# Attention inside one fused transformer kernel: V's products in five groups a pair instead of seven, a packed buffer for the turned probabilities, and a new order of the pair

## The chip, the cores and the metric

One core of a Trainium2 chip runs the whole program. The metric is device time in microseconds (us); lower is better. Engines: PE (TensorE) multiplies and transposes, ACT (ScalarE) does exponentials and copies, DVE (VectorE) does row extremes, rotations and copies, POOL (GpSimd) does wide additions, SP (SyncE) only issues DMAs. Each engine runs its own list of instructions in order and waits for the others through semaphores.

## The reference, cut to what matters

Half a feed-forward block, attention, half a feed-forward block, each behind a layer norm, on 4 sequences of 1024 tokens of width 128. The change touches the attention alone (16 heads of 64, causal, rotary):

```python
q = apply_rotary_emb(q, cos, sin)
k = apply_rotary_emb(k, cos, sin)
scores = jnp.einsum('bhid,bhjd->bhij', q, k) * scale
scores = jnp.where(causal, scores, -jnp.inf)
probs = jax.nn.softmax(scores, axis=-1)
out = jnp.einsum('bhij,bhjd->bhid', probs, v)
out = jnp.einsum('btd,od->bto', out.reshape(...), wo)
```

## The kernel before, in words

**The pair.** Attention runs over 32 pairs: one pair is two heads of one sequence. A loop body holds two pairs, u = 0 and u = 1; the first carries in addition the projection of V for the next four heads (`ahead_v`, four steps of six matmuls). The queries of a pair are taken in two groups of row blocks: g = 0 with blocks 0, 1, 6, 7 and g = 1 with blocks 2, 3, 4, 5; each group has eight score units (4 blocks, 2 heads). In the text `score(p,1,k)` is a unit of the running pair's group 1, `next_score(k)` one of the next pair's group 0.

**From scores to V.** PE writes the scores of a unit into a wide PSUM tile (L725, L726), DVE masks them and takes the row extreme (`max_of`, L1008), ACT takes the exponential and the row sum (`exponential`, L904). The probabilities are then transposed on PE (`turn(p,g,t)`, ten turns a group, L742) into one of two PSUM banks, the ring; ACT copies each turn into the SBUF tile `turned`, which lies in `shared_a` (`keep_turned`, L915), and V is multiplied with it (`times_v(p,...,g,d)`, L759). A product for key block j takes two matmuls, one a head, each with its 64 columns of the array, with as many moving columns as there are row blocks that see key block j. In the trace each such matmul has two rows, so that a pair of key blocks shows as x8. A ring bank is written again only when its last reader has released it (`may_write`, semaphore `ring_free`).

**Groups of products.** `times_v` is called seven times a pair: (0,0) to (0,3) for g = 0 with two key blocks each, (1,0) to (1,2) for g = 1.

**The row sums.** DVE inverts the sums (`invert`), PE transposes them (`turn_sums`, L768), ACT copies them to `inv_rows` (`keep_sums`, L923), SP writes them to DRAM (`send_inv`, L1183), waits for that, and reads them back spread over 64 partitions a head (`spread_inv`, L1191). DVE multiplies the output with them (`normalise`).

**Queries and keys two pairs ahead.** `ahead(0)` to `ahead(5)` project q and k of the pair after the next one (L120 to L122). DVE rotates each (`rope`), POOL adds and splits the halves, and SP, in the following pair, carries them by DMA to the tiles the scores read: `may_fill`, sixteen DMAs for `q_hl` and `k_hh` (L179, L180), `send_inv(p,0)`, two DMAs for `k_low` (L185). `next_score(0)` waits for all of these.

**SP's list.** It is strictly in order. In a pair: the sixteen fills, `send_inv(p,0)`, two `k_low` fills, `spread_inv(p,0)`, V and output weights; then, behind the end of `ahead(5)`, the weights `w_qk`, in pairs with u = 1 also `w_v` and the 1024 KB of `xn_cur`; then `send_inv(p,1)`, `spread_inv(p,1)`; then the next pair's fills.

The order of all engines in a pair is written by hand, one `pair` function for each engine.

Of the kernel before, what the change touches and what calls it, by code (L numbers as in the profile page):

```python
# [15 lines left out]
TOKENS = BATCH * SEQ  # L16
# [4 lines left out]
P = 128  # L21
# [4 lines left out]
ALL_PAIRS = BATCH * PAIRS  # L26
# [17 lines left out]
def some(count):  # L44


    return not isinstance(count, int) or count > 0
# [558 lines left out]
def attention(nc, x, xn_dram, xn_stored, inv_dram, wo_pairs, ahead_of, o, constants,  # L606
# [5 lines left out]
    with ctx:  # L612
# [20 lines left out]
        NK = sum(KEYS)  # L633
        TURNS = [[(0, (0,)), (0, (1,)), (1, (0,)), (1, (1,))] + [(j, (0, 1)) for j in range(2, 8)],
                 [(j, (h,)) for j in range(4) for h in range(2)] + [(4, (0, 1)), (5, (0, 1))]]
        RING = [[0, 1, 2, 3, 4, 5, 7, 9, 10, 11], [12, 13, 14, 15, 16, 17, 18, 19, 21, 23]]
        RING_SUM, RING_OUT = [6, 20], [22, 8]
# [5 lines left out]
        turned = turned_mem[:].rearrange("p (s c) -> p s c", s=4)  # L643
# [26 lines left out]
        def rows_at(g, j):  # L670
            return [r for r, block in enumerate(TILES[g]) if block >= j]

# [21 lines left out]
        def _(pe):  # L694
# [51 lines left out]
            def times_v(p, i, u, g, d):  # L746
                if d == 0:
                    if g == 0:
                        pe.wait_ge(v_copied[u], 16 * (i + 1))
                    if some(2 * p + g):  # L750
                        pe.wait_ge(head_done, 2 * p + g)
                ats = [at for at, (j, heads) in zip(RING[g], TURNS[g]) if j // 2 == d]
                for b in sorted({at % 2 for at in ats}):
                    pe.wait_ge(ring_free[b], bank_count(p, max(at for at in ats if at % 2 == b)))
                for j in (2 * d, 2 * d + 1):
                    w = P * len(rows_at(g, j))
                    slot = (NK * u + KEYS[0] * g + j) % 4
                    for h in range(2):
                        last = nc.tensor.matmul(out_bank[HEAD_DIM * h:HEAD_DIM * (h + 1), CHUNK - w:],  # L759
                                                v_cur[:, u, j, HEAD_DIM * h:HEAD_DIM * (h + 1)],  # L760
                                                turned[:, slot, h * w:(h + 1) * w], start=(j == 0), stop=(j == KEYS[g] - 1))
                    last.then_inc(out_step, 1)
# [14 lines left out]
            def pair(i, u, first, last):  # L777
                p = 2 * i + u
                has_prev, has_next, has_next2 = not (first and u == 0), not (last and u == 1), not last

                def ahead(n):
                    if has_next2:
                        project(i + 1, u, n)

                def ahead_v(n):
                    if has_next2 and u == 0:
                        project_v(i + 1, n)

                def next_score(k):
                    if has_next:  # L790
                        score(p + 1, i + u, 1 - u, 0, k)
                    elif k < 2:
                        if k == 1:
                            pe.wait_ge(early.centred_done, 1)
                        early_mean(nc, early, k, x, proj_bank)
                    elif k in (2, 4):
                        if k == 2:
                            pe.wait_ge(early.centred_done, 2)
                        else:
                            pe.wait_ge(early.ln_done, 1)  # L800
                        early_variance(nc, pe, early, k // 2 - 1, proj_bank)

                score(p, i, u, 1, 0)
                turn(p, 0, 0)
                turn(p, 0, 1)
                score(p, i, u, 1, 1)
                turn(p, 0, 2)
                ahead(0)
                if has_prev:
                    times_v(p - 1, i - 1 + u, 1 - u, 1, 2)  # L810
# [4 lines left out]
                turn_sums(p, 0)  # L815
                score(p, i, u, 1, 3)
                ahead(1)
                score(p, i, u, 1, 4)
# [66 lines left out]
            times_v(ALL_PAIRS - 1, ALL_PAIRS // 2 - 1, 1, 1, 2)  # L885
# [3 lines left out]
        def _(act):  # L889
# [17 lines left out]
            def keep_turned(p, u, g, t, signals=1):  # L907
                j, heads = TURNS[g][t]
                at, w = RING[g][t], P * len(rows_at(g, j))
                act.wait_ge(ring_full, ring_count(p, at))  # L910
                if some(NK * p + KEYS[0] * g + j - 3):
                    act.wait_ge(out_step, NK * p + KEYS[0] * g + j - 3)
                slot = (NK * u + KEYS[0] * g + j) % 4
                to = slice(heads[0] * w, (heads[-1] + 1) * w)
                nc.scalar.activation(turned[:, slot, to], ring[at % 2][:, 0:w * len(heads)],  # L915
                                     ACT.Copy).then_inc(ring_free[at % 2], signals)
# [8 lines left out]
            def pair(i, u, first, last):  # L925
                p = 2 * i + u
# [16 lines left out]
                keep_turned(p, u, 0, 1)  # L943
                exponential(p, 1, 0)
                keep_turned(p, u, 0, 2)
                exponential(p, 1, 1)
                keep_turned(p, u, 0, 3)
                keep_turned(p, u, 0, 4)
                keep_sums(p, 0, 1 if has_prev else 2)
                exponential(p, 1, 2)  # L950
                exponential(p, 1, 3)
                keep_turned(p, u, 0, 5)
# [5 lines left out]
                keep_turned(p, u, 0, 8)  # L958
                keep_turned(p, u, 0, 9)
                exponential(p, 1, 7)  # L960
                keep_turned(p, u, 1, 0)
                keep_turned(p, u, 1, 1)
                next_exponential(0)
                keep_turned(p, u, 1, 2)
                keep_turned(p, u, 1, 3)
# [11 lines left out]
                ahead_v(1)  # L977
                ahead_v(2)
                keep_turned(p, u, 1, 9)
                next_exponential(5)  # L980
                next_exponential(6)
                ahead_v(3)
# [12 lines left out]
        def _(dve):  # L995
# [16 lines left out]
            def keep_turned(p, u, g, t, signals=1):  # L1012
# [3 lines left out]
                if some(NK * p + KEYS[0] * g + j - 3):  # L1016
                    dve.wait_ge(out_step, NK * p + KEYS[0] * g + j - 3)
                slot = (NK * u + KEYS[0] * g + j) % 4
                to = slice(heads[0] * w, (heads[-1] + 1) * w)
                nc.vector.tensor_copy(turned[:, slot, to], ring[at % 2][:, 0:w * len(heads)]).then_inc(ring_free[at % 2], signals)  # L1020
# [22 lines left out]
            def pair(i, u, first, last):  # L1043
# [16 lines left out]

                max_of(p, 1, 0)
                max_of(p, 1, 1)
                invert(p, 0)
                ahead(0)
                max_of(p, 1, 2)
                if has_prev:
                    normalise(p - 1, 1)
                max_of(p, 1, 3)
# [6 lines left out]
                max_of(p, 1, 6)  # L1075
                max_of(p, 1, 7)
                ahead(3)
                invert(p, 1)
                next_max(0)
                ahead(4)  # L1080
                next_max(1)
                next_max(2)
                ahead(5)
# [5 lines left out]
                next_max(6)  # L1089
                next_max(7)  # L1090
# [335 lines left out]
```

## Time and profile before

| | |
|---|---|
| median of 3 runs | 1266.02 us (1262.96 to 1270.62) |
| profiled execution | 1268.34 us, of which the span shown is 1266.6 us |
| PE busy | 1221.1 us, 96% of the span |
| ACT, DVE, POOL busy | 891.7, 747.8, 405.3 us |
| POOL's three steps for one half of q and k (L153, L1133, L164), mean | 2.39, 1.04, 2.38 us |
| granted TensorE clock, mean | 0.990 |

A row of the timeline gives the start of an instruction, its duration, engine, line, operation and tiles. Matmuls are pipelined: the next one starts before the last one's modelled end, so a matmul's price is the distance from its start to the next start, not its duration. What stands in brackets is idle time before the instruction and what ended it.

### The profile page before, as it was taken

How to read it: one execution, taken by the hardware profiler on the slowest of the kernel's cores; microseconds unless marked ns; L12 is line 12 of the kernel's file. 1: busy time of each engine (PE TensorE's matmuls, PEld its weight loads, DVE VectorE, ACT ScalarE, POOL GpSimd, SP SyncE). 2: the span in 40 equal slices, each digit the busy share in tenths (PEclk: the TensorE clock that was granted, in tenths of full speed). 3: DMA queues.
4: the chain of work that ended last, by engine and by line, in shares of the span. 5: the costliest groups of instructions: out<-in, count | busy, mean ns of one | idle time of the engine just before them, and what ended most of it. 6: DMA issues, size and time to landing. Idle time of an engine off the chain costs nothing. (4 is left out here: it accounts for less than half of the span.)

```text
span 1266.6 us, 26505 instructions
## 1 busy us (share of the span) xinstructions
PE 1221.1 (96%) x7264; PEld 843.2 (67%) x7264; DVE 747.8 (59%) x1789; ACT 891.7 (70%) x1945; POOL 405.3 (32%) x224
## 2 busy tenths in 40 slices
PE   6996899999999999999999999999999999999898
PEld 3554577767677767777777767676767676766465
DVE  5575656565656565666566565656565656564454
ACT  4665577777777777777777777777777777777564
POOL 4134423333333333333333233333232333330000
PEclk8998899999999999999999999999999999999999
DMA  7125555545555555555555564656555455543000
GB/s 277 58 99 141 159 130 138 140 140 136 141 143 140 141 138 142 137 140 147 127 150 144 128 166 119 168 127 168 127 144 142 134 137 141 142 101 78 11 34 34
DMA packets 118608, 164.86 MB, mean 130 GB/s; under 512 B 14385, under 2 KB 64433, under 8 KB 118449
## 3 DMA queue, kind: packets, MB, share of 16 engines
q1 hardware_dynamic: 118176, 163.70, 48.4%
q10 hardware_dynamic: 400, 0.79, 0.3%
q8 instruction: 14, 0.23, 0.1%
q14 instruction: 18, 0.14, 0.0%
HBM read 53.02 MB, written 10.75 MB: 50 GB/s over the span
## 5 line engine op out<-in xcount | busy, mean ns | idle before, releaser
L1008 DVE CUSTOM_DVE_ANT_0 probs<-wide,tri_mask 128x1024 f32<-128x1024 f32 (+7 forms) x512 | 382.5, 755 | 249.2 <-PE wide L726 245.7
L904 ACT ACTIVATE probs<-probs,neg_max 128x1024 f32<-128x1024 f32 (+7 forms) x512 | 394.6, 772 | 85.1 <-DVE neg_max L1008 83.1
L915 ACT ACTIVATE shared_a<-bank 128x512 f32<-128x512 f32 (+2 forms) x640 | 338.2, 549 | 164.3 <-PE bank L742 158.4
L742 PEld LDWEIGHTS bank<-ident,probs 128*128 128x128 f32 x2304 | 259.3, 140 | 132.2 <-issue 70.1
L742 PE MATMUL bank<-ident,probs 128*128 128x128 f32 x2304 | 343.5, 278 | 1.1 <-ACT shared_a L915 0.4
L153 POOL TENSOR_TENSOR rotated<-terms,cross 128x1024 f32<-128x1024 f32 x62 | 148.4, 2394 | 610.8 <-DVE cross L147 610.6
L759 PE MATMUL bank<-shared_a,v_cur 128*64 128x256 f32 (+3 forms) x1792 | 297.3, 453 | 0.0
L725 PE MATMUL wide<-k_hh,q_hl 128*128 128x512 f32 (+3 forms) x768 | 287.8, 377 | 6.2 <-DMA k_low<-parts 4.6
L726 PE MATMUL wide<-k_low,q_hl 128*128 128x512 f32 (+3 forms) x768 | 254.8, 344 | 0.0
L759 PEld LDWEIGHTS bank<-shared_a,v_cur 128*64 128x64 f32 x1792 | 108.8, 136 | 121.9 <-issue 85.2
L725 PEld LDWEIGHTS wide<-k_hh,q_hl 128*128 128x128 f32 x768 | 145.9, 190 | 34.2 <-issue 21.8
L164 POOL TENSOR_TENSOR parts<-rotated,parts 128x1024 fp32r<-128x1024 f32 x64 | 152.3, 2380 | 9.5 <-ACT parts L158 0.5
L726 PEld LDWEIGHTS wide<-k_low,q_hl 128*128 128x128 f32 x768 | 146.5, 191 | 10.1
L904 ACT ACTIVATION_READ_ACCUMULATOR probs<-probs,neg_max 128x1 f32 x512 | 97.7, 191 | 0.0
L120 PE MATMUL bank<-xn_cur,w_qk 128*128 128x256 f32 (+1 forms) x192 | 70.4, 367 | 12.2 <-PEq L246 8.7
L1133 POOL CAST parts<-rotated 128x1024 fp32r<-128x1024 f32 x62 | 64.4, 1038 | 23.5 <-DMA k_low<-parts 13.6
L1040 DVE TENSOR_TENSOR x<-bank,x 128x256 f32 (+1 forms) x32 | 13.6, 425 | 95.4 <-PE bank L775 71.4
L775 PE MATMUL bank<-head_out,wo_cur 128*128 128x512 f32 x128 | 65.5, 593 | 1.2 <-DVE head_out L1031 1.2
L1037 DVE TENSOR_TENSOR x<-bank,x 128x512 f32 (+1 forms) x32 | 22.1, 692 | 68.1 <-PE bank L775 68.1
L122 PE MATMUL bank<-xn_cur,w_qk 128*128 128x256 f32 (+1 forms) x192 | 61.9, 322 | 0.0
L121 PE MATMUL bank<-xn_cur,w_qk 128*128 128x256 f32 (+1 forms) x192 | 61.5, 320 | 0.0
L299 PE MATMUL bank<-shared_a,w_down 128*128 128x512 f32 x96 | 50.0, 615 | 10.0 <-DVE shared_a L480 10.0
(142 smaller groups left out, 1257.0 us busy)
## 6 DMA issues: line engine op xcount, KB each, us to landing
q_hl<-parts SPq DMA_DIRECT2D x254, 128.0 KB, 2.8
k_hh<-parts SPq DMA_DIRECT2D x254, 128.0 KB, 2.7
v_cur<-shared_b SPq DMA_DIRECT2D x32, 512.0 KB, 4.3
inv_sum<-inv_scratch SPq DMA_DIRECT2D x128, 128.0 KB, 3.3
k_low<-parts SPq DMA_DIRECT2D x63, 256.0 KB, 4.1
xn_cur<-xn_scratch SPq DMA_DIRECT2D x15, 1024.0 KB, 7.0
w_qk<-w_scratch SPq DMA_DIRECT2D x32, 256.0 KB, 3.1
w_scratch<-first_w_parts SPq DMA_DIRECT2D x8, 512.0 KB, 3.1
```

Of the source, the lines that this page charges most:

```text
L120: nc.tensor.matmul(out[:, 0:w], w_qk[:, 0, half], xn_cur[:, 0, xs], start=True, stop=False)
L153: unit.tensor_tensor(o.rotated[:], o.terms[:], o.cross[:], ALU.add).then_inc(o.sum_done, 1)
L164: nc.gpsimd.tensor_tensor(o.parts[:, 1, :, cols], o.rotated[:], o.parts[:, 0, :, cols].bitcast(F32), ALU.subtract).then_inc(o.low_done, 1)
L725: nc.tensor.matmul(out, q, k_hh[u][h][:, keys], start=True, stop=False)
L726: last = nc.tensor.matmul(out, q, k_low[u][h][:, keys], start=False, stop=True)
L742: last = nc.tensor.transpose(ring[at % 2][:, col:col + P], probs[g][:, h, OFFSET[g][r] + j * P:OFFSET[g][r] + (j + 1) * P], ident[:])
L759: last = nc.tensor.matmul(out_bank[HEAD_DIM * h:HEAD_DIM * (h + 1), CHUNK - w:], v_cur[:, u, j, HEAD_DIM * h:HEAD_DIM * (h + 1)], turned[: ...
L775: nc.tensor.matmul(ring[at % 2][:], wo_cur[:, u, :], head_out[:], start=True, stop=True).then_inc(ring_full, 1)
L904: nc.scalar.activation(own, own, ACT.Exp, bias=neg_max[g][:, col], scale=-1.0, accum_out=sums[g][:, col]).then_inc(probs_done, 1)
L915: nc.scalar.activation(turned[:, slot, to], ring[at % 2][:, 0:w * len(heads)], ACT.Copy).then_inc(ring_free[at % 2], signals)
L1008: nc.vector.tensor_tensor_reduce(out=part_of_probs(g, k), in0=wide_banks[k % 2][:, x0:x1], in1=tri_mask[:, SEQ - (x1 - x0):], scale=1.0, s ...
L1133: nc.gpsimd.tensor_copy(o.parts[:, 0, :, cols], o.rotated[:]).then_inc(high_done, 1)
```

## The change

V's products are issued in five groups a pair: `GROUPS` gives for g = 0 the key blocks (0, 1), (2 to 5), (6, 7), for g = 1 (0, 1, 2), (3, 4, 5). The four equal slots of `turned` become places of each block's own width (`PLACE`), which lie from the other end of the tile in every second pair; `TAKEN` says how many products must be done before a place is written again. Three of the twenty copies of turned probabilities go from ACT to DVE. The order on PE, ACT and DVE is new.

```diff
+        GROUPS = [[(0, 1), (2, 3, 4, 5), (6, 7)], [(0, 1, 2), (3, 4, 5)]]
+        TAKEN = [[-3, -3, -4, 0, -1, -2, 1, 1], [2, 4, 6, 8, 9, 9]]
...
-        RING_SUM, RING_OUT = [6, 20], [22, 8]
+        RING_SUM, RING_OUT = [6, 20], [21, 8]
...
+        def place(u, g, j):
+            width = 2 * P * len(rows_at(g, j))
+            return PLACE[g][j] if u == 0 else TOKENS - PLACE[g][j] - width
...
-                for j in (2 * d, 2 * d + 1):
+                for j in GROUPS[g][d]:
                     w = P * len(rows_at(g, j))
-                    slot = (NK * u + KEYS[0] * g + j) % 4
+                    at = place(u, g, j)
```

PE's pair, from the running pair's score unit 6 of group 1 to the end of the next pair's early units, and then around the turned sums:

```diff
                 score(p, i, u, 1, 6)
-                times_v(p, i, u, 0, 1)
                 turn(p, 0, 8)
                 turn(p, 0, 9)
                 ahead(3)
                 score(p, i, u, 1, 7)
-                times_v(p, i, u, 0, 2)
                 turn(p, 1, 0)
                 next_score(0)
                 turn(p, 1, 1)
                 next_score(1)
+                times_v(p, i, u, 0, 1)
                 ahead(4)
                 turn(p, 1, 2)
                 turn(p, 1, 3)
-                times_v(p, i, u, 0, 3)
                 next_score(2)
                 ahead(5)
                 next_score(3)
+                times_v(p, i, u, 0, 2)
...
                 turn(p, 1, 7)
+                times_v(p, i, u, 1, 0)
                 turn_sums(p, 1)
-                times_v(p, i, u, 1, 0)
-                turn(p, 1, 8)
                 ahead_v(1)
                 project_out(p, i, u, 0, RING_OUT[0], p)
-                turn(p, 1, 9)
+                turn(p, 1, 8)
                 ahead_v(2)
                 next_score(6)
+                turn(p, 1, 9)
                 next_score(7)
-                times_v(p, i, u, 1, 1)
                 ahead_v(3)
```

ACT's pair around the copy of the sums, and DVE's pair at two of its three new copies:

```diff
+                next_exponential(3)
+                ahead_v(0)
+                keep_turned(p, u, 1, 7)
                 keep_turned(p, u, 1, 6)
-                ahead_v(0)
-                next_exponential(3)
-                keep_turned(p, u, 1, 7)
+                ahead_v(1)
                 keep_sums(p, 1)
...
                 max_of(p, 1, 6)
+                keep_turned(p, u, 0, 8)
                 max_of(p, 1, 7)
...
+                keep_turned(p, u, 1, 3)
                 next_max(3)
                 normalise(p, 0)
+                ahead(5)
```

What stands in the rows below: L752 of the changed file is the transpose (L742 before), L735 and L736 the scores, L769 the products with V, L778 the turned sums; in the order a group's matmuls are counted once, not by their two rows in the trace.

On PE, just before the next pair's first score, the kernel before has this in the pair with u = 1 (the last score of the running pair, the group (0,2), `turn(p,1,0)`, `next_score(0)`):

```order
L725 MATMUL wide<-k_hh,q_hl 128x384
L726 MATMUL wide<-k_low,q_hl 128x384
L759 MATMUL bank<-shared_a,v_cur 64x256 x4
L731 REGISTER_ALU
L742 MATMUL bank<-ident,probs 128x128 x4
L716 REGISTER_ALU
L717 REGISTER_ALU
L718 ISA
L725 MATMUL wide<-k_hh,q_hl 128x512
L726 MATMUL wide<-k_low,q_hl 128x512
```

The changed kernel, from the wait of `turn(p,1,1)` on, has the products of four key blocks behind the next pair's second score:

```order
L747 REGISTER_ALU
L752 MATMUL bank<-ident,probs 128x128 x4
L735 MATMUL wide<-k_hh,q_hl 128x512
L736 MATMUL wide<-k_low,q_hl 128x512
L735 MATMUL wide<-k_hh,q_hl 128x384
L736 MATMUL wide<-k_low,q_hl 128x384
L769 MATMUL bank<-shared_a,v_cur 64x256 x8
L711 REGISTER_ALU
L120 MATMUL bank<-xn_cur,w_qk 128x256
```

Two groups of products, with 256 columns each, have moved from the stretch before `next_score(0)` to the stretch behind it.

On PE, late in the same pair, the kernel before transposes the sums ahead of the group (1,0):

```order
L742 MATMUL bank<-ident,probs 128x128 x3
L766 REGISTER_ALU
L731 REGISTER_ALU
L768 MATMUL bank<-ident,inv 128x128
L759 MATMUL bank<-shared_a,v_cur 64x512 x4
L742 MATMUL bank<-ident,probs 128x128 x4
```

and the changed kernel behind it:

```order
L752 MATMUL bank<-ident,probs 128x128 x3
L769 MATMUL bank<-shared_a,v_cur 64x512 x6
L776 REGISTER_ALU
L741 REGISTER_ALU
L778 MATMUL bank<-ident,inv 128x128
L785 MATMUL bank<-head_out,wo_cur 128x512
```

The group is longer by a key block, and the sums now come after it.

On DVE, between the extremes of the running pair's last two score units, a copy out of the ring has come in:

```order
L1012 ISA probs,neg_max<-wide,tri_mask 128x512
L1012 ISA neg_max 128x1
L1019 REGISTER_ALU
L1021 ISA
L1023 COPY shared_a<-bank 128x512
L1007 REGISTER_ALU
L1012 ISA probs,neg_max<-wide,tri_mask 128x384
```

This copy releases the ring bank that `turn(p,1,0)` writes next; before, it was ACT's.

## Rows read from the trace of the kernel before

**Rows 1.** PE's timeline, transposed sums (L768) of two pairs, 28 pairs apart.

```profile
181.79 0.30 PE L768 MATMUL bank<-ident,inv 128*128 128x128 f32 x1
1106.72 0.33 PE L768 MATMUL bank<-ident,inv 128*128 128x128 f32 x1
```

**Rows 2.** PE's timeline, groups of V's products and what stands beside them.

```profile
614.40 0.40 PE L725 MATMUL wide<-k_hh,q_hl 128*128 128x512 f32 x1
614.63 0.40 PE L726 MATMUL wide<-k_low,q_hl 128*128 128x512 f32 x1
614.96 1.08 PE L759 MATMUL bank<-shared_a,v_cur 128*64 128x256 f32 x8
615.98 0.88 PE L742 MATMUL bank<-ident,probs 128*128 128x128 f32 x6
...
621.33 0.60 PE L742 MATMUL bank<-ident,probs 128*128 128x128 f32 x4
621.68 0.48 PE L725 MATMUL wide<-k_hh,q_hl 128*128 128x512 f32 x1
...
629.77 1.94 PE L759 MATMUL bank<-shared_a,v_cur 128*64 128x512 f32 x8
631.64 0.66 PE L742 MATMUL bank<-ident,probs 128*128 128x128 f32 x4
632.05 0.36 PE L129 MATMUL bank<-w_v,xn_cur 128*128 128x256 f32 x1
...
632.85 1.02 PE L775 MATMUL bank<-head_out,wo_cur 128*128 128x512 f32 x2
```

**Rows 3.** PE's timeline over one loop body: end of ahead(5), sums, first scores.

```profile
592.86 0.28 PE L122 MATMUL bank<-xn_cur,w_qk 128*128 128x256 f32 x1
...
596.47 0.27 PE L768 MATMUL bank<-ident,inv 128*128 128x128 f32 x1
...
620.30 0.49 PE L725 MATMUL wide<-k_hh,q_hl 128*128 128x512 f32 x1 [0.79 <-DMA k_low<-parts]
...
625.28 0.28 PE L122 MATMUL bank<-xn_cur,w_qk 128*128 128x256 f32 x1
...
654.11 0.66 PE L742 MATMUL bank<-ident,probs 128*128 128x128 f32 x4
654.52 0.47 PE L725 MATMUL wide<-k_hh,q_hl 128*128 128x512 f32 x1
...
659.47 0.28 PE L122 MATMUL bank<-xn_cur,w_qk 128*128 128x256 f32 x1
...
685.86 0.47 PE L725 MATMUL wide<-k_hh,q_hl 128*128 128x512 f32 x1
```

**Rows 4.** SP's timeline in the same stretch: DMA issues.

```profile
597.33 0.27 SPq L1183 DMA_DIRECT2D inv_scratch<-inv_rows  x1
602.28 1.15 SPq L1191 DMA_DIRECT2D inv_sum<-inv_scratch  x2
604.12 0.59 SPq L179 DMA_DIRECT2D q_hl<-parts  x1
...
614.96 1.18 SPq L185 DMA_DIRECT2D k_low<-parts  x2
...
630.60 0.29 SPq L1183 DMA_DIRECT2D inv_scratch<-inv_rows  x1
631.87 1.14 SPq L1191 DMA_DIRECT2D inv_sum<-inv_scratch  x2
633.21 0.59 SPq L179 DMA_DIRECT2D q_hl<-parts  x1
```

**Rows 5.** DVE's timeline, extreme of the unit score(p,1,6).

```profile
651.27 0.68 DVE L1008 CUSTOM_DVE_ANT_0 probs<-wide,tri_mask 128x512 f32<-128x512 f32 x1
```

**Rows 6.** Busy time by stretch: us, then busy time by engine, granted clock, DMA share, GB/s.

```profile
136.00:140.00 4.00, 3.22 (x11) 2.50 (x9) 1.93 (x7) 0.99 (x4) 3.82 (x2) 0.57 0.59 172
949.00:955.00 6.00, 4.78 (x35) 3.93 (x35) 3.81 (x8) 3.14 (x7) 3.43 (x2) 1.00 0.62 163
```

More of the change, by code:

```diff
@@ L642, in attention @@
         probs = [sb(f"probs{g}", [P, 2, WIDTH]) for g in range(2)]
-        turned = turned_mem[:].rearrange("p (s c) -> p s c", s=4)
+        turned = turned_mem[:]
         neg_max, sums = ([sb(f"{n}{g}", [P, 8]) for g in range(2)] for n in ("neg_max", "sums"))
@@ L671, in rows_at, with steps_before @@
             return [r for r, block in enumerate(TILES[g]) if block >= j]
+        def place(u, g, j):
+            width = 2 * P * len(rows_at(g, j))
+            return PLACE[g][j] if u == 0 else TOKENS - PLACE[g][j] - width
+        def steps_before(p, g, j):
+            return NK * p + TAKEN[g][j]
         def unit(p, g, k):
@@ L751, in times_v @@
                         pe.wait_ge(head_done, 2 * p + g)
-                ats = [at for at, (j, heads) in zip(RING[g], TURNS[g]) if j // 2 == d]
+                ats = [at for at, (j, heads) in zip(RING[g], TURNS[g]) if j in GROUPS[g][d]]
                 for b in sorted({at % 2 for at in ats}):
                     pe.wait_ge(ring_free[b], bank_count(p, max(at for at in ats if at % 2 == b)))
-                for j in (2 * d, 2 * d + 1):
+                for j in GROUPS[g][d]:
                     w = P * len(rows_at(g, j))
-                    slot = (NK * u + KEYS[0] * g + j) % 4
+                    at = place(u, g, j)
                     for h in range(2):
@@ L760, in times_v @@
                                                 v_cur[:, u, j, HEAD_DIM * h:HEAD_DIM * (h + 1)],
-                                                turned[:, slot, h * w:(h + 1) * w], start=(j == 0), stop=(j == KEYS[g] - 1))
+                                                turned[:, at + h * w:at + (h + 1) * w], start=(j == 0), stop=(j == KEYS[g] - 1))
                     last.then_inc(out_step, 1)
@@ L804, in pair @@
                 turn(p, 0, 0)
+                score(p, i, u, 1, 1)
                 turn(p, 0, 1)
-                score(p, i, u, 1, 1)
                 turn(p, 0, 2)
@@ L809, in pair @@
                 if has_prev:
-                    times_v(p - 1, i - 1 + u, 1 - u, 1, 2)
+                    times_v(p - 1, i - 1 + u, 1 - u, 1, 1)
                 turn(p, 0, 3)
@@ L814, in pair @@
                 turn(p, 0, 5)
-                turn_sums(p, 0)
                 score(p, i, u, 1, 3)
                 ahead(1)
+                turn_sums(p, 0)
                 score(p, i, u, 1, 4)
@@ L910, in keep_turned @@
                 act.wait_ge(ring_full, ring_count(p, at))
[L911 to L915, printed above, removed]
+                if some(steps_before(p, g, j)):
+                    act.wait_ge(out_step, steps_before(p, g, j))
+                to = slice(place(u, g, j) + heads[0] * w, place(u, g, j) + (heads[-1] + 1) * w)
+                nc.scalar.activation(turned[:, to], ring[at % 2][:, 0:w * len(heads)],
                                      ACT.Copy).then_inc(ring_free[at % 2], signals)
@@ L948, in pair @@
                 keep_turned(p, u, 0, 4)
+                keep_turned(p, u, 0, 5)
                 keep_sums(p, 0, 1 if has_prev else 2)
@@ L951, in pair @@
                 exponential(p, 1, 3)
-                keep_turned(p, u, 0, 5)
                 exponential(p, 1, 4)
@@ L976, in pair @@
                 keep_turned(p, u, 1, 8)
-                ahead_v(1)
                 ahead_v(2)
-                keep_turned(p, u, 1, 9)
                 next_exponential(5)
+                ahead_v(3)
                 next_exponential(6)
-                ahead_v(3)
             for k in range(7):
@@ L1015, in keep_turned @@
                 dve.wait_ge(ring_full, ring_count(p, at))
[L1016 to L1020, printed above, removed]
+                if some(steps_before(p, g, j)):
+                    dve.wait_ge(out_step, steps_before(p, g, j))
+                to = slice(place(u, g, j) + heads[0] * w, place(u, g, j) + (heads[-1] + 1) * w)
+                nc.vector.tensor_copy(turned[:, to], ring[at % 2][:, 0:w * len(heads)]).then_inc(ring_free[at % 2], signals)
             def invert(p, g):
@@ L1075, in pair @@
                 max_of(p, 1, 6)
+                keep_turned(p, u, 0, 8)
                 max_of(p, 1, 7)
-                ahead(3)
                 invert(p, 1)
                 next_max(0)
+                ahead(3)
+                next_max(1)
                 ahead(4)
-                next_max(1)
                 next_max(2)
-                ahead(5)
+                keep_turned(p, u, 1, 3)
                 next_max(3)
                 normalise(p, 0)
+                ahead(5)
                 next_max(4)
@@ L1089, in pair @@
                 next_max(6)
+                keep_turned(p, u, 1, 9)
                 next_max(7)
```

15 lines of the change are left out of this document (7 added, 8 removed).

## The prediction, made before the changed kernel was run

> **What bounds the kernel now.** The mean period of a loop body (two pairs) comes first: 28 pairs, 14 bodies, take 1106.72 - 181.79 = 924.9 us, 66.07 us a body [rows 1]. Next I read PE's timeline through one body and marked two events: the last matmul of `ahead(5)`, call it X, and the first matmul of `next_score(0)`, call it N. In order they are X (u = 1) at 592.86, N (u = 0) at 620.30, X (u = 0) at 625.28, N (u = 1) at 654.52, X at 659.47, N at 685.86 [rows 3]. So a body has four stretches: A, from X of u = 1 to N of the next body; 4.98 us; B, 29.24 us; 4.95 us. The last three add up to 39.17, which leaves 66.07 - 39.17 = 26.90 for A on average.
>
> The N that closes A is the one that waits. In the first A it stood for `k_low`; that A took 27.44 us, the second, which waits for nothing, 26.39 [rows 3]. So PE alone would need 26.39 + 39.17 = 65.56 a body, the N that waits costs 0.5 more, and two paths of nearly equal length lead through A: PE's own work, and a chain of DMAs.
>
> That chain I read on SP's timeline [rows 4]. Behind X come the weights and `xn_cur`, then the sums go to DRAM at 597.33; their read-back is issued at 602.28 (4.95 us later, against 630.60 to 631.87, 1.27 us, in u = 0, where no `xn_cur` goes ahead of them); the first fill at 604.12; `k_low` at 614.96; N at 620.30. From the read-back to N is 18.02 us, of which 10.84 are the issuing of the sixteen fills. N - X on average less 18.02 puts the read-back 8.9 us behind X. The rest of the chain is SP's strict order, and nothing PE does makes it shorter.
>
> **The change part by part.** *Price of a group.* Two key blocks with 512 columns each take 631.64 - 629.77 = 1.87, two with 256 take 615.98 - 614.96 = 1.02 [rows 2]. The difference, 0.85, is two times 256 columns, so 0.85 is also what the columns of the shorter one cost, and 0.17 is the group's own. The matmul ahead of it takes 0.33 where its equal takes 0.23; four transposes behind it take 0.41 against 0.35 [rows 2]. That is 0.33; where a score follows, its second matmul is late as well, so I take 0.36. Two groups fewer: 0.72 a pair, 23 us over 32 pairs, if PE sets the pace.
>
> *Where the work goes.* Group (0,1) of the new division (four key blocks with 256 columns, 4 x 0.425 = 1.70) moves from before N to between N and X. Its last group, key blocks 6 and 7 (384 columns, 0.64), moves from there to behind X. So the two short stretches each grow by 1.06, to 6.04 and 6.01, while their number of groups stays one. A and B lose 1.06 of columns and two groups of six: 1.78 each. PE would reach N 24.6 us behind X in A, and take 27.5 in B.
>
> *The sums.* This is the step that I think decides. `turn_sums(p,1)` went behind the group (1,0), which has grown by a key block, and behind the group (0,2), which now lies after X. In A it stands 596.47 - 592.86 = 3.61 behind X now [rows 3]. Added: 384 columns and a group, 0.64 + 0.33; 3 x 512 columns and a group, 2.55 + 0.33. That makes 7.5. From the transpose to the DMA's issue took 0.86 (597.33 less 596.47), so the issue comes at 8.3, and with 1.27 for the way to DRAM the read-back at 9.6. In this body it was at 9.4, on average at 8.9: `xn_cur` covers most of the delay, not all. I take 9.5, so A = 9.5 + 18.0 = 27.5, where PE is ready at 24.6. PE then waits 2.9 us, less what other waits inside A take of it.
>
> In B nothing large goes ahead of the sums. There the transposed sums wait for `ahead_v(0)` too (six projections, 632.85 - 632.05 = 0.80 [rows 2]): 8.3 behind X. ACT now copies `ahead_v(1)` before the sums: another 0.80 and part of a copy, then 0.86. Issue at 9.9 to 10.4, I take 9.9; read-back 11.2; first fill 1.34 later (631.87 to 633.21); `k_low` 10.84 after that; N another 5.34 (614.96 to 620.30) [rows 3, 4]. That is 28.7, where PE would be ready at 27.5. A chain with slack now binds.
>
> *The copies that go to DVE.* ACT loses three, which is worth nothing, since no term above is ACT's work. The copy behind `score(p,1,6)` is new in front of `turn(p,1,0)`. DVE ends that unit's extreme at 651.95 [rows 5]; the copy itself has no row in this trace: the same engine's pass over 512 columns, 0.68, is the nearest, zero the other end. It would end by 652.6, while `turn(p,1,0)`, which starts at 654.11 behind two groups (2 x 1.18) that are gone, could start at 651.8 [rows 3]. So up to 0.8 of waiting, ahead of N in both halves. In A the DMA chain covers it; in B it lifts PE's 27.5 to 28.3, still under 28.7. If the chain in B were shorter, it would be the next in line. The copy in front of `next_max(3)`, with `normalise` ahead of the last `rope`, brings POOL's halves 1 to 2 us later; they must be there by the first fill, 11 us behind X, and an end of `rope` 3 us behind X leaves 8 for POOL, whose three steps take 5.8 (the table of the profile): no cost.
>
> *The places of `turned`.* Same columns, other addresses: nothing on PE, ACT or DVE. Its new waits name products that stand earlier in PE's order than the turns which they hold back: nothing.
>
> *Sum.* 27.5 + 6.04 + 28.7 + 6.01 = 68.25 us a body against 66.07: 2.2 more. Fourteen bodies make 30.5; the first and the last pair, without such a chain, give back 0.72 each. So +29 on the profiled 1268.34 (span 1266.6), and, since that stands 2.3 above the median of 1266.02, 1295 on the scale of the median.
>
> [...]
>
> **The rivals.** *PE sets the pace after all:* the groups' 0.72 a pair come out in full, 1266 - 23 = 1243. For it: PE is busy 96% of the span and N waits for only 0.5 a body. Against: A's chain, 26.9, is longer than PE's 26.4 today, and PE's road through A shrinks while work moves to the stretch behind N. It needs a chain that gets 2 us shorter.
>
> *The change doesn't do what it says, because A's chain keeps its length and B stays PE's:* 26.9 + 6.04 + 27.5 + 6.01 = 66.45, 0.4 a body, +4 with the ends: 1270. The saving in A is lost to the wait, and the one in B goes into the two stretches. For it: `xn_cur` may hide the late sums altogether.
>
> *Only one chain is late:* A at 27.5 and B at 27.5 make 67.05, +13 with the ends: 1279. It needs ACT to reach the sums in B 1.2 us sooner than I have it.
>
> *The waits cost clock:* worst of all, on the slower side beyond mine. At 131 to 140 us, where PE stands for stretches of up to 3 us, the granted clock of 136 to 140 is 0.57, near the lower of its levels (1.2 of 2.4 GHz); in 949 to 955, with the longest wait at N, it is 1.00 [rows 6]. Fourteen waits of up to 2.9 us lie between. If each brought 4 us at 0.57, 1.7 of work would be lost each time, 24 in all: 1319. The Trainium skill (TensorE: Matmul & The Clock Gate, HAM oscillation) says that waits for DMA between bursts of matmuls can do this; here only the start of the program shows it.
>
> **How the numbers follow.** Both chains late 0.64, at 1295, its own range 1284 to 1308. One chain late 0.13. Chain unchanged 0.08. PE's pace 0.08. Clock lost 0.07. The range 1267 to 1308 leaves out the fast case, the clock case and little else. A measurement of this kernel can tell a change of about 0.5%, 6.3 us, from none: faster 0.08, same 0.08 (1270 lies in it), slower 0.84.
>
> **What would show it.** In the trace of the changed kernel N should carry a wait for `k_low` in every body, of 2 us or more at u = 0 and of up to 1 at u = 1; the sums should be sent 8 us behind X instead of 4.5; the read-back should follow 1.3 us later; X to N should be 27 to 28 and 28 to 29 us, and a body 68. There should be five groups a pair, each with the same 0.17 of its own. `turn(p,1,0)` should wait for DVE. I am wrong if N starts without waiting, if the read-back follows X in less than 9 us, or if the body's period falls below 66.

## The result and the profile after

The changed kernel takes 1313.28 us (median; 1305.93 to 1319.97) against 1265.53 for the kernel before: ratio 1.037, 95% interval 1.034 to 1.041. The direction was right; the time is 18.3 us above the forecast and 5 above its range. The profiled execution took 1305.93 us (span 1304.2).

PE's timeline in the profiled execution: sums of two pairs, 28 pairs apart, then X and N over one body, as in [rows 1, 3].

```profile
178.61 0.27 PE L778 MATMUL bank<-ident,inv 128*128 128x128 f32 x1
...
606.29 0.28 PE L122 MATMUL bank<-xn_cur,w_qk 128*128 128x256 f32 x1
...
613.63 0.33 PE L778 MATMUL bank<-ident,inv 128*128 128x128 f32 x1
...
633.55 0.49 PE L735 MATMUL wide<-k_hh,q_hl 128*128 128x512 f32 x1 [1.13 <-DMA k_low<-parts]
...
639.60 0.28 PE L122 MATMUL bank<-xn_cur,w_qk 128*128 128x256 f32 x1
...
668.34 0.49 PE L735 MATMUL wide<-k_hh,q_hl 128*128 128x512 f32 x1
...
674.69 0.28 PE L122 MATMUL bank<-xn_cur,w_qk 128*128 128x256 f32 x1
...
702.09 0.49 PE L735 MATMUL wide<-k_hh,q_hl 128*128 128x512 f32 x1 [1.28 <-DMA k_low<-parts]
...
1138.55 0.27 PE L778 MATMUL bank<-ident,inv 128*128 128x128 f32 x1
```

| us | before | forecast | after |
|---|---|---|---|
| A, X (u = 1) to N | 26.9 mean | 27.5 | 27.3, N waits |
| N to X (u = 0) | 4.98 | 6.04 | 6.05 |
| B, X (u = 0) to N | 29.24 | 28.7 | 28.74, N does not wait |
| N to X (u = 1) | 4.95 | 6.01 | 6.35 |
| body | 66.07 | 68.25 | 68.4 in most; mean of 14, (1138.55 - 178.61)/14 = 68.57 |

The row to look at is N at 668.34: it has no bracket. A is closed by the DMA, as forecast; B is closed by PE.

SP's timeline of the same body, as in [rows 4].

```profile
614.29 0.27 SPq L1189 DMA_DIRECT2D inv_scratch<-inv_rows  x1
615.54 1.15 SPq L1197 DMA_DIRECT2D inv_sum<-inv_scratch  x2
617.38 0.59 SPq L179 DMA_DIRECT2D q_hl<-parts  x1
...
628.22 1.18 SPq L185 DMA_DIRECT2D k_low<-parts  x2
...
649.49 0.29 SPq L1189 DMA_DIRECT2D inv_scratch<-inv_rows  x1
650.77 1.13 SPq L1197 DMA_DIRECT2D inv_sum<-inv_scratch  x2
652.10 0.59 SPq L179 DMA_DIRECT2D q_hl<-parts  x1
...
662.95 1.18 SPq L185 DMA_DIRECT2D k_low<-parts  x2
```

In A the sums go 614.29 - 606.29 = 8.0 behind X and the read-back 9.25 (forecast 8.3 and 9.5), in B 9.9 and 11.2 (forecast 9.9 and 11.2). From `k_low` to N are 633.55 - 628.22 = 5.33 in A; in B the same 5.34 would give 668.29, and PE is there at 668.34. So B's chain is as long as forecast, but PE arrives with it and not 0.4 to 1.2 earlier.

What delays PE stands in the groups of the profile's page (columns: busy time and mean ns; idle time before them, and what ended most of it):

```profile
L735 PE MATMUL wide<-k_hh,q_hl 128*128 128x512 f32 (+3 forms) x768 | 293.9, 383 | 22.5 <-DMA k_low<-parts 20.6
...
L120 PE MATMUL bank<-xn_cur,w_qk 128*128 128x256 f32 (+1 forms) x192 | 74.3, 387 | 25.5 <-DVE cross L147 13.4
```

The first line is the forecast wait at N (6.2 before). The second wasn't forecast: `ahead(3)` stands for DVE, some 30 times. DVE's timeline there:

```profile
664.56 0.69 DVE L1040 TENSOR_TENSOR x<-bank,x 128x512 f32 x1 [2.13 <-PE bank L785]
665.17 0.81 DVE L1012 CUSTOM_DVE_ANT_0 probs<-wide,tri_mask 128x640 f32<-128x640 f32 x1
...
665.91 0.42 DVE L146 TENSOR_TENSOR cross<-bank,cos 128x256 f32<-128x256 f32 x1
666.25 0.41 DVE L147 SCALAR_TENSOR_TENSOR cross<-bank,sin 128x256 f32<-128x256 f32 x1
666.58 0.68 DVE L1012 CUSTOM_DVE_ANT_0 probs<-wide,tri_mask 128x512 f32<-128x512 f32 x1
...
667.18 0.69 DVE L1023 COPY shared_a<-bank 128x512 f32<-128x512 f32 x1
```

Behind `project_out` DVE has 3.3 us of work without a gap: the addition to x, a maximum, `ahead(2)`'s rope, a maximum, the new copy. All projections share one bank, so `ahead(3)` can't start before the rope of `ahead(2)` has read it (666.6). In the kernel before, the group (0,1) [rows 2, 614.96 to 615.98] stood between the two, and needs nothing of DVE. That group is what the change carries behind N.

*Where the 48 us are.* The first X and the last, in the profile before, in the one after, and in that of a second series of the changed kernel:

```profile
163.44 0.28 PE L122 MATMUL bank<-xn_cur,w_qk 128*128 128x256 f32 x1
...
1122.63 0.28 PE L122 MATMUL bank<-xn_cur,w_qk 128*128 128x256 f32 x1
```

```profile
158.52 0.28 PE L122 MATMUL bank<-xn_cur,w_qk 128*128 128x256 f32 x1
...
1153.55 0.28 PE L122 MATMUL bank<-xn_cur,w_qk 128*128 128x256 f32 x1
```

```profile
164.49 0.28 PE L122 MATMUL bank<-xn_cur,w_qk 128*128 128x256 f32 x1
...
1160.52 0.28 PE L122 MATMUL bank<-xn_cur,w_qk 128*128 128x256 f32 x1
```

The third execution (1313.23 us, span 1311.5) stands for the median. Against the one before: 1.0 us up to the first X, 996.0 - 959.2 = 36.8 between the marks (14.5 bodies), and 151.0 - 144.0 = 7.0 behind the last X; together the 44.9 by which it is longer than 1268.34. The profiled execution is shorter chiefly by its start, 6.0 us: there the granted clock is 0.91 in its first 40 us and from 130 to 150, where the third has 0.87 and 0.74.

### The profile page after: what moved, and what is told of

Same layout as the page of the kernel before. It is cut to its first block and busy times, and to the rows that moved or that the text cites. A ratio compares the mean times of both kernels' runs of the same rounds, so it can differ in the third digit from the quotient of the medians.

```text
span 1304.2 us, 26489 instructions
## 1 busy us (share of the span) xinstructions
PE 1223.6 (94%) x7264; PEld 851.3 (65%) x7264; DVE 801.8 (61%) x1885; ACT 847.1 (65%) x1849; POOL 405.5 (31%) x224
## 5 line engine op out<-in xcount | busy, mean ns | idle before, releaser
L922 ACT ACTIVATE shared_a<-bank 128x512 f32<-128x512 f32 (+2 forms) x544 | 291.3, 555 | 154.6 <-PE bank L752 150.3
L752 PE MATMUL bank<-ident,probs 128*128 128x128 f32 x2304 | 342.0, 278 | 6.7 <-DVE x L1044 3.2
L752 PEld LDWEIGHTS bank<-ident,probs 128*128 128x128 f32 x2304 | 261.1, 141 | 111.1 <-issue 43.8
L735 PE MATMUL wide<-k_hh,q_hl 128*128 128x512 f32 (+3 forms) x768 | 293.9, 383 | 22.5 <-DMA k_low<-parts 20.6
L769 PE MATMUL bank<-shared_a,v_cur 128*64 128x256 f32 (+3 forms) x1792 | 283.3, 449 | 1.8 <-DVE shared_a L1023 1.8
L736 PE MATMUL wide<-k_low,q_hl 128*128 128x512 f32 (+3 forms) x768 | 258.0, 344 | 0.0
L769 PEld LDWEIGHTS bank<-shared_a,v_cur 128*64 128x64 f32 x1792 | 114.5, 136 | 123.4 <-issue 92.3
L735 PEld LDWEIGHTS wide<-k_hh,q_hl 128*128 128x128 f32 x768 | 146.4, 191 | 39.1 <-issue 16.3
L736 PEld LDWEIGHTS wide<-k_low,q_hl 128*128 128x128 f32 x768 | 147.2, 192 | 10.0
L120 PE MATMUL bank<-xn_cur,w_qk 128*128 128x256 f32 (+1 forms) x192 | 74.3, 387 | 25.5 <-DVE cross L147 13.4
L903 ACT ACTIVATE shared_b<-bank 128x512 f32<-128x512 f32 x60 | 35.5, 592 | 50.0 <-PE bank L131 49.4
L120 PEld LDWEIGHTS bank<-xn_cur,w_qk 128*128 128x128 f32 x192 | 36.3, 189 | 47.1 <-DVE cross L147 20.7
L122 PE MATMUL bank<-xn_cur,w_qk 128*128 128x256 f32 (+1 forms) x192 | 62.0, 323 | 0.0
```

Source lines behind the costliest of these rows:

```text
L120: nc.tensor.matmul(out[:, 0:w], w_qk[:, 0, half], xn_cur[:, 0, xs], start=True, stop=False)
L735: nc.tensor.matmul(out, q, k_hh[u][h][:, keys], start=True, stop=False)
L736: last = nc.tensor.matmul(out, q, k_low[u][h][:, keys], start=False, stop=True)
L752: last = nc.tensor.transpose(ring[at % 2][:, col:col + P], probs[g][:, h, OFFSET[g][r] + j * P:OFFSET[g][r] + (j + 1) * P], ident[:])
L922: nc.scalar.activation(turned[:, to], ring[at % 2][:, 0:w * len(heads)], ACT.Copy).then_inc(ring_free[at % 2], signals)
```

## The experiments

All ratios are to the kernel before, run beside them. Medians of the kernel before were 1264.99, 1264.53 and 1264.61 in the three series.

**The changed kernel again**, unedited, for a second trace.

> The changed kernel once more, unchanged, to see how far its own executions lie apart. Its profiled execution had a body of 68.4 us, a granted clock of 1.00 inside the loop and 0.990 on average, and 1305.9 us; its other executions had mean clocks of 0.981 to 0.987 and 1311.9 to 1320.0 us. Theory (chains and waits, with some clock lost on top): times between 1305 and 1320, and the slower ones have the lower mean clock, about 1.3 us for each 0.001 of it. Rival (the spread is DMA latency alone): the mean clock does not go with the time. If a profiled execution here has less than 1.00 inside the loop, the stretch where it falls should lie behind N at u = 0, the longest wait of PE.

1313.81 us, 1.038 (1.035 to 1.041). As expected; its trace is used above.

**Sums back ahead of the group.**

```
  turn(p, 1, 7)
+ turn_sums(p, 1)
  times_v(p, i, u, 1, 0)
- turn_sums(p, 1)
```

> The changed kernel with one step undone: the sums of group 1 are transposed ahead of the group (1,0) again, and ACT copies them before the copy of ahead_v(1). Theory (the late sums make the chains late and hold up ACT at the end of the pair): the sums are sent about 5.5 us behind X instead of 8, A falls from 27.3 to about 26.8 (xn_cur then bounds the read-back), and the waits at the end of the u = 0 pair (0.14 and 0.40 us) go; 0.5 to 1.0 us a body, 7 to 14 us in all, 1299 to 1306. Rival (the late sums are covered and the cost sits in the groups and copies themselves): no change within 0.5%, 1307 to 1320.

1296.89 us, 1.026 (1.023 to 1.028); 17 less than the changed kernel, a little more than expected. ACT's copies were put in the matching order. A falls to between 25.9, without a wait at N, and 27.4; B from 28.74 to 28.56. So the late sums make about a third of the 48 us, and PE's own road through A is 25.9, not the 24.6 of the prediction. B's chain is early here. SP's timeline, and PE's at N:

```profile
656.64 1.18 SPq L185 DMA_DIRECT2D k_low<-parts  x2
```

```profile
664.29 0.48 PE L735 MATMUL wide<-k_hh,q_hl 128*128 128x512 f32 x1
```

With X at 635.74, `k_low` goes 20.9 behind X instead of 23.35, so with the 5.34 from there to N the chain would let N start at 26.2; it starts at 28.55. In this run PE, with its waits for DVE and ACT, closes B, and no DMA does.

**Late sums alone**, in the kernel before.

```
- turn_sums(p, 1)
  times_v(p, i, u, 1, 0)
+ turn_sums(p, 1)
```

> The kernel before with the turned sums behind the group (1,0) and nothing else. Theory, that xn_cur's transfer covers the delay until about 8 us behind X: the sums are sent 6.7 behind X instead of 4.5, the read-back stays at 9 to 9.5, A 26.5 to 27.4 and B 29.25 as before, time 1264 to 1270. Rival, that the chain grows by all of the delay: read-back at 11.1, A 29.1, time 1265 + 2.2 x 14.5 = 1297.

1281.60 us, 1.013 (1.010 to 1.016): between the two, and by neither mechanism. In A the read-back stays 7.7 to 9.5 behind X, as the first theory said, but A is 27.15 with N *not* waiting, and B grew from 29.25 to 29.74. PE's timeline behind the sums:

```profile
606.34 0.33 PE L768 MATMUL bank<-ident,inv 128*128 128x128 f32 x1
...
607.02 1.13 PE L775 MATMUL bank<-head_out,wo_cur 128*128 128x512 f32 x2
608.63 0.44 PE L742 MATMUL bank<-ident,probs 128*128 128x128 f32 x2 [0.48 <-ACT shared_a L915]
```

The transposed sums now meet the transposes behind them in the two turning banks, and PE waits for ACT's copies. A step in the strict order has two costs, the chain it starts and the bank it holds; I had priced the first.

**The sums on another queue**, in the kernel before: sent from ACT's queue, not behind `xn_cur`'s transfer on SP's.

```
  nc.scalar.activation(inv_rows[g][:], ...)
+ if g == 1:
+     act.wait_ge(ring_free[at % 2], bank_count(p, at))
+     act.dma_start(inv_dram[g], inv_rows[g][:]).then_inc(inv_sent[g], 16)
...
- send_inv(p, 1)
```

> The kernel before with one edit: the sums of group 1 go to DRAM from ACT's own DMA queue, right behind their copy, instead of from SP's, where they stand behind xn_cur. Theory (A is a chain of DMAs whose first link is the wait of the sums behind xn_cur): the read-back is issued about 6 us behind X instead of 8.9, or at the latest when the queue is free; fills start when POOL's halves are there, 7.5 to 8 us behind X; N no longer waits, the body is 65.6 instead of 66.1: 5 to 8 us less, 1258 to 1261. Rival (the queue does not matter, the DMA engines are shared): A stays at 26.9, 1266.

1262.45 us, 0.998 (0.996 to 1.000): not clear of the noise, where 5 to 8 us were expected. The trace shows what the time can't. ACT's and SP's timelines:

```profile
597.09 0.27 ACTq L926 DMA_DIRECT2D inv_scratch<-inv_rows  x1
```

```profile
600.50 1.15 SPq L1194 DMA_DIRECT2D inv_sum<-inv_scratch  x2
```

With X at 592.63 the read-back is 7.9 behind X (9.4 in [rows 4]); even on a queue of its own a 4 KB write takes 3.4 us to its read-back beside `xn_cur`'s transfer (3.2 to 4.5 over the bodies), against 1.27 in B. From the third body on A is 26.4 with no wait at N, the body 65.57. That is PE's own time of [rows 3], now in nearly every body.

**The changed kernel without its chain in A**: sums early and on ACT's queue.

> The changed kernel with the turned sums back ahead of the group (1,0) and the sums of group 1 sent from ACT's queue. Theory, that A is set by the DMA chain and that what is left of the loss is PE's waits for DVE and ACT: A 25.9 with 0 to 0.4 of waiting, B 28.56 as before, short stretches 6.05 to 6.37, body 66.9, time 1285 (1281 to 1289) against 1296.9 with the sums turned early alone; and if it is the waits at N that cost clock, the mean granted clock is 0.988 or more in each execution. Rival, that PE's other waits take what the wait at N gives back: 1294 to 1298.

1293.07 us, 1.022 (1.019 to 1.025); only 4 less than with early sums alone, not clear of the noise, and nearer the rival. But for the first body A is 26.0 to 26.5, yet the stretch behind N of u = 0, 6.05 before, is now up to 6.37: where N doesn't stand, `turn(p,1,1)` stands for the exponential instead. The expectation about the clock missed too: two executions of four are at 0.985 and 0.986. So with the chain gone the five groups are still 28 us slower than before, and what is left is PE waiting for DVE and ACT.

**Five groups in the old order**: (0,1) where (0,2) stood, ahead of N; (0,2) where (0,3) stood; the old (1,1) gone; the copies on ACT as before.

```
  score(p, i, u, 1, 6)
- times_v(p, i, u, 0, 1)
...
  score(p, i, u, 1, 7)
- times_v(p, i, u, 0, 2)
+ times_v(p, i, u, 0, 1)
...
- times_v(p, i, u, 0, 3)
+ times_v(p, i, u, 0, 2)
...
- times_v(p, i, u, 1, 1)
  ahead_v(3)
```

> The kernel before with the five groups and the packed, mirrored places alone; the order of everything else stays, (0,1) stands where (0,2) stood, ahead of N, (0,2) where (0,3) stood, the old (1,1) is gone. No copy goes to DVE. Theory: each group saves 0.36 us, so B shrinks from 29.25 to 28.5, the two short stretches stay at 4.97, and A stays with its DMA chain at about 26.9 while PE would be ready at 25.7; body 65.3, 0.75 less than before, 10 to 13 us: 1253 to 1256. Rival 1 (fewer groups are worth nothing, or packing costs): 1266 or more. Rival 2 (no chain, PE sets the pace): 23 us less, 1243.

1294.10 us, 1.024 (1.022 to 1.026) where 1253 to 1256 was expected: the clearest miss. PE's timeline at the place where the group is gone:

```profile
662.15 0.82 PE L752 MATMUL bank<-ident,probs 128*128 128x128 f32 x6
663.42 0.50 PE L120 MATMUL bank<-xn_cur,w_qk 128*128 128x512 f32 x1 [0.46 <-DVE cross L147]
```

The same `ahead(3)` in the kernel before, behind the six transposes at 615.98 in [rows 2]:

```profile
616.61 0.47 PE L120 MATMUL bank<-xn_cur,w_qk 128*128 128x512 f32 x1
```

663.42 - 662.15 = 1.27 for six transposes that take 616.61 - 615.98 = 0.63 there: 0.64 lost where the group saved 0.36. Similar waits, for DVE's maximum and ACT's exponentials, came where (1,1) stood. N does not wait in most bodies and the body is 67.9. Against PE's 65.56 that is 1.2 more a pair: two groups fewer took 0.72 off PE's work and brought some 1.9 of waits that they had hidden. The other half of rival 1, that packing costs, has no sign in the trace: between 300 and 1090 us neither ACT nor DVE waits for a product before it writes a place.

**The columns moved back ahead of N**, in the changed kernel: (0,1) behind `score(p,1,6)`, (0,2) between N and X.

```
  score(p, i, u, 1, 6)
+ times_v(p, i, u, 0, 1)
...
  next_score(1)
- times_v(p, i, u, 0, 1)
  ahead(4)
  turn(p, 1, 2)
  turn(p, 1, 3)
+ times_v(p, i, u, 0, 2)
...
  next_score(3)
- times_v(p, i, u, 0, 2)
```

> The changed kernel with the four-key group (0,1) back ahead of N (behind score(p,1,6)) and the last group (0,2) back between N and X. Theory, that N in A stands for the DMA chain and columns put behind N are paid in full, and that ahead(3) waits 0.65 us for DVE only because no products stand ahead of it: short stretches 4.97 and about 5.3 (from 6.06 and 6.35), A 26.6 to 27.0, B 28.74 + 2.06 - 0.97 - 0.65 = 29.2, body 66.2, time 1313.8 - 2.2 x 14.5 = about 1282 (1278 to 1286). Rival, that DMA chains decide A and B alike: A 26.9, B 28.6, body 65.5, time 1271. Rival, that the place of the columns is all one and the waits lie elsewhere: body 68.4, time 1311 to 1315.

1342.36 us, 1.062 (1.060 to 1.065): 29 worse than the changed kernel, where 32 better was expected, and outside both rivals. The short stretches are 6.7 to 7.1 although they lost columns. PE's timeline:

```profile
652.83 0.34 PE L736 MATMUL wide<-k_low,q_hl 128*128 128x384 f32 x1
654.63 0.39 PE L120 MATMUL bank<-xn_cur,w_qk 128*128 128x256 f32 x1 [1.47 <-DVE terms L143]
```

The change has also moved the rope of `ahead(3)` behind `next_max(0)`, and the group (0,1) in its new place is the cover of that rope; taken out, `ahead(4)` waits about 1.7 us in every pair. The columns behind N are not simply paid in full, as the prediction had it: they hide DVE there, as they did ahead of N.

**The rope ahead of the maximum**, on DVE in the changed kernel.

```
+ ahead(2)
  max_of(p, 1, 5)
- ahead(2)
```

> The changed kernel with one swap on DVE: the rope of ahead(2) goes ahead of max_of(p,1,5). Theory, that PE's own waits (ahead(3) for that rope, 0.65 us a pair) set B, and the DMA chain sets A: B 28.74 becomes 28.1, in A the wait at N grows from 1.4 to 2.0 and A stays 27.3, body 67.8, time 1313.8 - 0.65 x 14.5 = about 1304 (1302 to 1307). Rival, that a DMA chain sets B too, as forecast: nothing changes, 1311 to 1316.

1309.12 us, 1.036 (1.033 to 1.039), between theory and rival and hardly clear of the changed kernel. The wait of `ahead(3)` is gone, B is still 28.76 and the 4 us come from elsewhere (`turn(p,1,1)`; the last stretch is 6.07, not 6.35). PE's timeline in A; in B the same wait is 0.60:

```profile
632.06 0.48 PE L120 MATMUL bank<-xn_cur,w_qk 128*128 128x512 f32 x1
...
633.99 0.66 PE L752 MATMUL bank<-ident,probs 128*128 128x128 f32 x4 [0.59 <-DVE shared_a L1023]
```

This is `turn(p,1,0)` waiting for the copy on DVE, the step that the prediction named with "up to 0.8". In the changed kernel the wait of `ahead(3)` hides it: PE is held once, by DVE's 3.3 us, wherever it first asks. N does not wait in B, so what kept B is this wait. The rival, a chain in B, isn't ruled out by this run: the chain ends within 0.1 us of PE, and would have held N in its place.

**The copy behind `score(p,1,6)` back on ACT.**

> The changed kernel with the copy behind score(p,1,6) back on ACT. Theory: DVE has 0.3 us of idle time behind that copy and no instruction of PE waits for it there, so nothing changes: 1309 to 1317. Rival, the step of the prediction that this copy delays turn(p,1,0) by up to 0.8 us ahead of N: B 28.0 and 1302.

1318.88 us, 1.043 (1.040 to 1.047), 5 worse, where no change was expected. PE's timeline, u = 0:

```profile
640.15 0.66 PE L752 MATMUL bank<-ident,probs 128*128 128x128 f32 x4 [0.69 <-ACT shared_a L922]
...
641.19 0.49 PE L735 MATMUL wide<-k_hh,q_hl 128*128 128x512 f32 x1 [0.38 <-DMA k_low<-parts]
```

ACT is later with that copy than DVE, and `turn(p,1,0)` stands 0.8 us longer in both halves. This tells the two stretches apart: B went from 28.74 to 29.54, all of it (the stretch behind it gave 0.3 back), while A stayed at 27.27 and the wait at N shrank from 1.4 to 0.6. A is closed by the DMA chain. In B the chain is no later than PE; that PE closes B even without the chain is shown by the run with the sums back ahead, where `k_low` came 2.45 us earlier and B lost only 0.18.

**Four places put back together**: columns, sums, rope and queue.

> The changed kernel with four places put back: the four-key group ahead of N and the last group between N and X, the turned sums ahead of the group (1,0), the rope of ahead(2) ahead of max_of(p,1,5), and the sums of group 1 sent from ACT's queue. Theory (chain in A, PE's waits in B, ends some 7 us longer): A 26.3 without a wait at N, short stretches 5.0 and 5.3, B 29.0, body 65.6, time about 1266 (1262 to 1271). Rival, that fewer groups bring new waits of PE for ACT's copies at the seam of the pairs, as with the five groups in the old order: body 66.8 or more, 1283 or more.

1343.17 us, 1.064 (1.060 to 1.067), where about 1266 was expected. It has the fault of the columns run: `ahead(4)` waits for the rope of `ahead(3)`, and the short stretches are mostly 6.7 to 7.1. The time lies where the rival had it, but the wait is for DVE and not for ACT.

**Six groups**, in the kernel before with the sums on ACT's queue: blocks 2 to 5 as one group at the old place of blocks 2 and 3, so that `ahead(3)` keeps its cover.

```
+ GROUPS = [[(0, 1), (2, 3, 4, 5), (6, 7)], [(0, 1), (2, 3), (4, 5)]]
...
  score(p, i, u, 1, 7)
- times_v(p, i, u, 0, 2)
  turn(p, 1, 0)
...
- times_v(p, i, u, 0, 3)
+ times_v(p, i, u, 0, 2)
```

> The kernel before with one group fewer (key blocks 2 to 5 as one group, at the place of the old group of blocks 2 and 3, so that ahead(3) keeps its cover; group 1 keeps its three groups) and with the sums of group 1 sent from ACT's queue. Theory, that a group is worth 0.36 us where it covered no wait: body 65.57 - 0.72 = 64.85, N without a wait, time 1262.5 - 0.72 x 14.5 = about 1252 (1249 to 1256). Rival, that a group taken away brings a wait in its place wherever it stood, as in the five groups in the old order: 1260 to 1275.

1268.09 us, 1.003 (1.002 to 1.004). Where N doesn't wait, A and B lose 0.3 each, about as expected, and the short stretches gain 0.4; in other bodies A is up to 28.4 and N waits for `k_low` again. PE's timeline:

```profile
652.91 0.40 PE L727 MATMUL wide<-k_low,q_hl 128*128 128x512 f32 x1
653.52 0.55 PE L743 MATMUL bank<-ident,probs 128*128 128x128 f32 x3 [0.21 <-ACT probs L904]
```

The group that stood behind `score(p,1,7)` had covered the road from that score over its maximum and its exponential to `turn(p,1,1)`.

**Six groups, with a score put into the gap.**

```
  next_score(0)
- turn(p, 1, 1)
  next_score(1)
+ turn(p, 1, 1)
```

> The kernel before with six groups and with the sums of group 1 sent from ACT's queue, as in the run of that name, and turn(p,1,1) moved behind next_score(1). Theory, that the 0.4 us which the six groups lost behind N was turn(p,1,1) standing for score(p,1,7), its maximum and its exponential, which the group taken away had covered, and that a score now covers it: short stretches 4.97, A 26.1 plus up to 0.5 of waiting for the chain, B 28.95, body 64.9 to 65.3, time 1252 to 1258. Rival, that DVE sets the pace behind N and the wait moves on to ahead(4) or next_score(2): 1265 to 1269 as without the swap.

1260.44 us, 0.997 (0.996 to 0.999), over 12 runs; the body is 65.44. This is 0.3% faster than the kernel before, by 4 us where 7 to 13 were expected: 8 us of the wait came back, but A is 26.34, not 26.1, with 0.1 to 0.2 each of new waits for a maximum and a turning bank. It doesn't separate from the kernel with the other queue alone (1262.45, in another series), so that fewer groups gain anything in the time isn't shown.

## Why the prediction was wrong

*Price of a group: right, and no use alone.* The six groups took 0.3 out of A and of B, near the 0.36. The step that failed is the next one, "A and B lose 1.06 of columns and two groups of six: 1.78 each. PE would reach N 24.6 us behind X in A, and take 27.5 in B." It treats the products as work and not as cover. PE's road is 25.9 in A and 28.74 in B. For B the difference of 1.24 is three waits in the trace after: `ahead(3)` 0.70, `ahead_v(3)` for ACT's copy 0.40, `turn(1,8)` for the sums' copy 0.14. They don't simply add: with the last two all but gone (sums back ahead) B lost 0.18. Over a body in which nothing waits for a DMA, that run has PE at 25.91 + 6.35 + 28.56 + 6.35 = 67.2, where the prediction's figures for PE add up to 64.15 and the kernel before took 65.56: even with the sums back ahead the change makes PE's own road longer, not shorter. The profile before could have shown the first wait. DVE's timeline there, the last step of that rope:

```profile
615.68 0.42 DVE L147 SCALAR_TENSOR_TENSOR cross<-bank,sin 128x256 f32<-128x256 f32 x1
```

It ends at 616.1 and PE asks for it at 616.61, so 1.02 of products stand over 0.5 of slack.

*The sums in A: right*, to 0.3 us in each of their times, and A came out at 27.3 for 27.5. N waits 1.4 and not 2.9 (the prediction asked for 2 or more), because other waits inside A have taken the rest; the prediction allowed for that and the copy run shows it.

*B: right number, by luck.* The chain of 28.7 is there, but PE's 28.74 closes B, and N starts without waiting, which the prediction named as a sign of being wrong. With the chain 2.45 us earlier B is still 28.56. That the two meet within 0.1 us hid the failed step: the body came out at 68.4 for 68.25.

*N to X: right for u = 0* (6.05 for 6.04); for u = 1 0.34 short, `turn(p,1,1)` waiting for the exponential.

*The copy on DVE: right in kind.* Its wait of up to 0.8 exists, but is hidden behind that of `ahead(3)`, as the rope run shows.

*The ends: mis-sized.* "The first and the last pair, without such a chain, give back 0.72 each" was -1.4; behind the last X it is +7.0. The last loads have a chain too, and without projections PE has less to put beside it. PE's timeline there, in the profile after; the kernel before has neither wait:

```profile
1180.70 0.77 PE L735 MATMUL wide<-k_hh,q_hl 128*128 128x512 f32 x1 [2.66 <-DMA k_low<-parts]
...
1228.88 1.52 PE L769 MATMUL bank<-shared_a,v_cur 128*64 128x384 f32 x12 [1.77 <-DVE shared_a L1023]
```

The first is the last N. Behind it the granted clock is 0.57 from 1180 to 1182 and 0.58 from 1182 to 1184 us, some 1.7 of work lost; with the 2.66 and the 1.77 that is most of the 7.0. The longer end comes with the new order, the copies on DVE among it, and neither with five groups alone nor with the late sums: behind the last X there are 144.2 us with five groups in the old order, as before (144.0), and 151.7 with the sums back ahead.

*The sum.* Of the 18.3 us by which the time missed, 8.4 are the ends, 6.3 the stretch between the marks (36.8 for 30.5: bodies of 68.4, half a body more than counted, and first bodies of 69 to 71), 1.0 the start and 2.3 that I moved the sum down to the median's scale, which the changed kernel's traces don't follow.

*The clock rival (0.07) holds in single bodies.* Busy time by stretch in the rope run (us, busy by engine, granted clock, DMA share, GB/s):

```profile
428.00:430.00 2.00, 0.41 (x2) 0.38 (x3) 0.20 (x1) 0.89 (x3) 0.43 (x1) 1.00 0.84 247
430.00:432.00 2.00, 2.00 (x10) 1.72 (x9) 0.99 (x1) 0.00 (x0) 1.85 (x2) 0.67 0.97 228
432.00:434.00 2.00, 2.00 (x10) 1.09 (x10) 2.00 (x5) 1.66 (x3) 1.13 (x1) 0.50 0.00 0
434.00:436.00 2.00, 2.00 (x19) 1.32 (x16) 0.45 (x2) 0.06 (x1) 0.00 (x0) 0.98 0.00 0
```

PE stood 0.6 us ahead of `turn(p,1,0)` and 1.8 at N (429.58); then the clock is granted at 0.50, its lower level, and the stretch to X takes 7.65 instead of 6.07. The Trainium skill (TensorE: Matmul & The Clock Gate, HAM oscillation) has such a loss behind waits between bursts; this trace agrees, while the profile after holds 1.00 in the whole loop, through thirteen gaps ahead of N of 1.4 to 2.4 us. The second trace of the changed kernel, the run without the chain and the copy run have one such body each, the run of four places three, each 1.5 to 1.9 us. So in the loop it is 0 to 5 us a run, not the 24 of the rival.

*Open:* how much of the scatter between executions of the changed kernel (mean granted clock 0.990 at 1305.93, 0.981 at 1319.97) lies in the start and how much in the loop; only executions with a trace could be split.

## What to carry to other kernels

Before moving or merging work that waits for nobody, look up what the other engines do while it runs: it is the cover of their latency, and its price is not its own time but the wait that stands bare without it. Check at both places, the old and the new, when the result that the next instruction needs is ready (DVE's rope 0.5 us early under 1.02 of products), and do it for the bodies at the ends as well. To see which of two paths of equal length closes a stretch, delay one by a known amount and, in another run, make the other one early: the path that binds lets the delay through in full and doesn't follow the other.

## What the runs showed that was not expected

- A 4 KB write that shares the chip with `xn_cur`'s 1 MB load needs 3.2 to 4.5 us from issue to read-back on a queue of its own, and 1.27 without that load.
- One gap can hold several waits: removing the one with the name (0.7 for DVE's rope) gave back nothing, since the next (0.6 for DVE's copy) stood behind it.
- The granted clock fell to 0.50 with no wait at N too, in the run of four places, behind 1.4 us of PE standing for DVE's rope.
